# Turning the gated attention output by DMA instead of on TensorE, with a new order of work in the attention groups

## The reference

```python
h = _layernorm(x) * (1 + ca) + sa
xn = h / norm(h) * scale * gamma                # _L0_attn_ref
q, kv, a = split(einsum('bnd,ed->bne', xn, W_qkva), 3)
a = sigmoid(a)
y = scan over n:  y[n] = a[n] * y[n-1] + kv[n]
x = x + ga * (q * y)
h = _layernorm(x) * (1 + cb) + sb
x = x + gb * fp4_linear(silu(fp4_linear(h, w_gate)) * fp4_linear(h, w_up), w_down)
```

## Time and profile before

| | before |
|---|---|
| median of 3 executions | 1963.17 us |
| the profiled execution | 1961.58 us |
| its span, first to last instruction | 1959.8 us |
| busy in the span: TensorE | 1936.3 us (99%) |
| VectorE | 1686.6 us (86%) |
| ScalarE | 629.5 us (32%) |
| GpSimd | 1198.9 us (61%) |
| mean granted TensorE clock | 0.998 of full speed |

### The profile page before, as it was taken

How to read it: one execution, slowest core, us unless ns; L and a number is a source line. 1 busy time by engine, 2 the same in 40 slices (tenths; PEclk the granted TensorE clock), 3 DMA queues, 4 the chain that set the end, 5 groups by cost and what they waited for, 6 DMA issues and landing times.

```text
span 1959.8 us, 27185 instructions
## 1 busy us (share of the span) xinstructions
PE 1936.3 (99%) x9403; PEld 927.2 (47%) x9403; DVE 1686.6 (86%) x2106; ACT 629.5 (32%) x885; POOL 1198.9 (61%) x1072
## 2 busy tenths in 40 slices
PE   8999999999999999999999999999999999999998
PEld 3444444444444444444444444444444444444444
DVE  7786767676868999999999999999999999999986
ACT  4333433343413233233233323323232332322221
POOL 1554764546535777677667667767766776776641
PEclk9999999999999999999999999999999999999999
DMA  8866665757552433433433343343334334333323
GB/s 292 272 178 144 174 170 149 174 142 200 125 129 69 108 74 80 98 75 72 92 89 72 81 100 74 74 94 88 73 84 96 72 76 97 80 72 87 88 62 77
DMA packets 421251, 218.22 MB, mean 111 GB/s; under 512 B 359858, under 2 KB 359870, under 8 KB 421188
## 3 DMA queue, kind: packets, MB, share of 16 engines
q1 hardware_dynamic: 421188, 217.39, 45.1%
HBM read 95.43 MB, written 33.57 MB: 66 GB/s over the span
## 4 chain that ended last, share of the span: by engine, by line
PE 87%; DVE 6%; issue 2%; POOL 2%; DMA 1%; ACT 1%; SPq 1%; DVEq 0%; POOLq 0%
PE bank L1067 43%; PE bank L986 20%; PE bank L1087 15%; PE bank L1091 7%; PE bank L1011 1%; SPq L398 1%; DVE arena L1163 1%; DMA arena<-arena 1%; DVE bn L1152 1%; DVE arena L1292 0%; DMA arena<-in_L_attn_x_dram 0%; DVE arena L1454 0%; PE bank L925 0%; DMA arena<-in_L_ffn_w_up_dram 0%; DVE arena L1461 0%
## 5 line engine op out<-in xcount | busy, mean ns | idle before, releaser
L1067 PE MATMUL bank<-wgu_hi,arena 128*128 128x512 f16 (+1 forms) x3072 | 869.9, 362 | 2.0 <-DVE arena L1401 2.0
L1067 PE MATMUL bank<-wgu_lo,arena 128*128 128x512 f16 (+1 forms) x1536 | 555.7, 362 | 0.0
L986 PE MATMUL bank<-arena,wq_hi 128*128 128x512 f16 x1536 | 458.5, 380 | 2.3 <-DMA arena<-arena 1.3
L1067 PEld LDWEIGHTS bank<-wgu_hi,arena 128*128 128x128 f16 x3072 | 300.5, 98 | 310.1 <-issue 2.4
L986 PE MATMUL bank<-arena,wq_lo 128*128 128x512 f16 x768 | 292.3, 381 | 0.0
L1087 PE MATMUL bank<-wd_hi,arena 128*128 128x512 f16 x693 | 263.0, 379 | 0.1
L1087 PE MATMUL bank<-wd_lo,arena 128*128 128x512 f16 x693 | 263.0, 380 | 0.0
L986 PEld LDWEIGHTS bank<-arena,wq_hi 128*128 128x128 f16 x1536 | 150.0, 98 | 178.4 <-issue 3.7
L1067 PEld LDWEIGHTS bank<-wgu_lo,arena 128*128 128x128 f16 x1536 | 150.2, 98 | 153.7
L663 POOL TENSOR_TENSOR arena<-arena 128x512 f32<-128x512 f32 x63 | 153.2, 2431 | 95.4 <-DVE arena L1476 95.4
L1401 DVE SCALAR_TENSOR_TENSOR arena<-bank,small,arena 128x512 f32<-128x512 f32 (+1 forms) x192 | 134.1, 701 | 85.8 <-PE bank L1067 81.5
(11 more groups left out here) (162 smaller groups left out, 2743.6 us busy)
## 6 DMA issues: line engine op xcount, KB each, us to landing
arena<-in_L_attn_x_dram SPq DMA_DIRECT2D x32, 1024.0 KB, 5.9
arena<-x_scratch SPq DMA_DIRECT2D x128, 256.0 KB, 3.2
x_scratch<-arena SPq DMA_DIRECT2D x16, 1024.0 KB, 4.4
out_dram<-arena SPq DMA_DIRECT2D x64, 256.0 KB, 3.1
arena<-in_L_wmod_dram SPq DMA_DIRECT2D x6, 1024.0 KB, 14.4
arena<-arena SPq DMA_TRANSPOSE x258, 3.5
wgu_hi<-in_L_ffn_w_gate_dram SPq DMA_DIRECT2D x1, 2816.0 KB, 12.3
wgu_lo<-in_L_ffn_w_up_dram SPq DMA_DIRECT2D x1, 2816.0 KB, 19.0
```

The source lines that it names most:

```text
L986: last = pe.matmul(dst[m % 2][:, :].rearrange("p (j t) -> p j t", j=NJ), w[:, k, at], uT[p][:, half, :, k, :], start=(n == 0), stop=(n == ...
L1067: last = pe.matmul(dst[n][:, 0:w], xT[p][:, half, k, :], wt[:, k, cut], start=(m == 0), stop=(m == 3 * KD - 1))
```

## The change

The mix product is no longer turned on TensorE. VectorE writes it over the decay buffer (float32, channels on partitions). ScalarE copies it as 16-bit integers into two planes, the low and the high half of each float32 (`split_mix`, 1024 elements an instruction, four a group). When the four chunks of a group are split, SP issues one DMA transpose of 32 blocks of 128x128 16-bit elements (`turn_mix`). ScalarE puts the planes together again into float32 rows (`join_mix`, one instruction for each of the four row blocks), and `add_x` reads these from SBUF instead of PSUM. The state is kept in two buffers instead of four, and its last column is copied into a small `carry` tile after each scan.

```diff
+                def turn_mix(i):
+                    sp.wait_ge(mix_split, CH * (i + 1))
+                    wait(sp, mix_joined, NJ * i)
+                    sp.dma_start(mixT_bits..., mix_bits..., transpose=True).then_inc(mixT_loaded, 16)
...
                 def decays(i, m):
                     act.wait_ge(a_ready, CH * i + m + 1)
-                    wait(act, state_ready, CH * i + m - 1)
+                    wait(act, mix_split, CH * i + m - 1)
...
+                def split_mix(i, m):
+                    act.wait_ge(mix_ready, CH * i + m + 1)
+                    wait(act, mixT_loaded, 16 * i)
+                    act.activation(mix_bits[:, :, :, m, :], decay[m % 2].bitcast(U16)..., ACT.Copy).then_inc(mix_split, 1)
+
+                def join_mix(i, js):
+                    act.wait_ge(mixT_loaded, 16 * (i + 1))
+                    for j in js:
+                        wait(act, x1_ready, NJ * i + j - 1)
+                        act.activation(mix_rows[j % 2].bitcast(U16)..., mixT_bits[:, :, j, :]..., ACT.Copy).then_inc(mix_joined, 1)
...
                 def mix(i, p, b, m, first):
+                    if not first:
+                        dve.wait_ge(carry_ready, CH * (i - 1) + m + 1)
-                    dve.tensor_tensor_scan(state[m], ..., 0.0 if first else state[m][:, GT - 1:GT], ...)
+                    dve.tensor_tensor_scan(state[m % 2], ..., 0.0 if first else carry[:, m:m + 1], ...)
+                    dve.tensor_copy(carry[:, m:m + 1], state[m % 2][:, GT - 1:GT]).then_inc(carry_ready, 1)
-                    dve.scalar_tensor_tensor(mixT[p][:, m, :], q_bank[m % 2][:, :], ...)
+                    dve.scalar_tensor_tensor(decay[m % 2], q_bank[m % 2][:, :], ...)
...
-                        dve.tensor_tensor(xr[:, j, :], t_bank[j % 2][:, :], xr[:, j, :], ALU.add)
+                        dve.tensor_tensor(xr[:, j, :], mix_rows[j % 2], xr[:, j, :], ALU.add)
```

More of the change, by code:

```diff
@@ L176, in adaln_block_kernel @@
         used[0] -= B * KD * P + CH * B
-        state = [view(GT) for _ in range(CH)]
+        state = [view(GT) for _ in range(2)]
+        mix_rows = [view(D) for _ in range(2)]
         xs[0] = view(NJ * D).rearrange("p (j d) -> p j d", j=NJ)
@@ L846, in group @@
-                    decays(i, 1)
-                    if more:
-                        squares(i + 1, 1 - p, (2, 3))
-                        u_hi(i + 1, 1 - p)
-                    else:
+                        decays(i, 1)
+                        split_mix(i, 0)
+                        weights(0)
+                        join_mix(i - 1, (2, 3))
                         steps_of_x(0, 0)
                         x_hi(0, 0)
+                        weights(1)
+                        decays(i, 2)
@@ new lines, in group @@
+                        split_mix(i, 1)
+                        weights(2)
+                        ffn_apply(2, 0)
+                        steps_of_x(1, 1)
+                        decays(i, 3)
+                        split_mix(i, 2)
+                        x_hi(1, 1)
+                        ffn_apply(3, 1)
+                        weights(3)
+                        return
+                    squares(i + 1, 1 - p)
+                    u_hi(i + 1, 1 - p)
+                    join_mix(i - 1, (0, 1))
@@ L865, in group @@
+                    weights(2)
+                    decays(i, 3)
+                    split_mix(i, 2)
                     weights(3)
                 groups(group)
+                split_mix(NGA - 1, 3)
                 silu(0, 0, 0, 0)
@@ L881, in tile @@
                         x_hi(3, 1)
+                        join_mix(NGA - 1, range(NJ))
                         return
@@ L1286, in finish_modulation @@
                                            ALU.mult))
+                carry = col("gamma_q", KD)
                 def mix(i, p, b, m, first):
@@ L1514, in group @@
                     mix(i, p, b, 0, first)
+                    if not more:
+                        add_x(i - 1, (0, 1))
+                        first_stats(0)
+                        first_stats(1)
+                        finish_modulation()
+                        weights(0)
+                        add_x(i - 1, (2, 3))
+                        mix(i, p, b, 1, first)
+                        quantise_x(0, 0)
+                        first_stats(2)
+                        x_lo(0, 0)
+                        weights(1)
+                        mix(i, p, b, 2, first)
+                        weights(2)
+                        quantise_x(1, 1)
+                        mix(i, p, b, 3, first)
+                        x_lo(1, 1)
+                        first_stats(3)
+                        weights(3)
+                        return
+                    if two_more:
+                        stats_mean_var(i + 2, p)
                     add_x(i - 1, (0, 1))
+                    u_lo(i + 1, 1 - p)
+                    mix(i, p, b, 1, first)
+                    weights(0)
+                    add_x(i - 1, (2, 3))
                     if i == 1:
@@ L1518, in group @@
                         weight_max(3, raw_down[1])
-                    if not more:
-                        first_stats(0)
-                        first_stats(1)
-                        finish_modulation()
-                    weights(0)
-                    add_x(i - 1, (2, 3))
-                    mix(i, p, b, 1, first)
-                    if two_more:
-                        stats_mean_var(i + 2, p)
-                    if more:
-                        u_lo(i + 1, 1 - p)
-                    else:
-                        quantise_x(0, 0)
-                        first_stats(2)
-                        x_lo(0, 0)
-                    if i == 1:
                         diagonal(t_bank[0], wmax_turned, wmax_diagonal)
@@ L1541, in group @@
                     weights(2)
-                    if not more:
-                        quantise_x(1, 1)
                     mix(i, p, b, 3, first)
-                    if not more:
-                        x_lo(1, 1)
-                        first_stats(3)
                     weights(3)
@@ L1606, in tile @@
                         x_lo(3, 1)
+                        add_x(NGA - 1, range(NJ))
                         return
```

96 lines of the change are left out of this document (47 added, 49 removed).

## The result

The changed kernel takes 2023.0 us (median of 4 runs, 2022.4 to 2025.7), beside 1963.3 for the kernel before on the same chip: ratio 1.031, 95% interval 1.0289 to 1.0325. The forecast was 1986, the range 1966 to 2006. The direction was right, the size was not. The profiled execution took 2025.7, its span is 2023.9.

A forecast was written before the change was run, and what follows sets the result against it. TensorE, busy 1936.3 of 1959.8 us, was taken as the bound. Delays of 15.3 by group 15, 7.3 at attention's end and 1.5 in the FFN made 24.1 on 1961.58: 1985.7, said as 1986, range 1966 to 2006.

The forecast's parts named there:

- From group 7 on ... no wait. So groups 7 to 14 each win 1.74: Steady attention groups: TensorE never waits, so each group saves its two transpose batches, 1.74 us.
- 1.5 lost: Groups 11 to 14: w_down tiles 1408 wide instead of 1024 eat 2 us of slack; 1.5 us lost.
- Mix(i,1) was put at T + 21: Steady groups, T being the group's start on TensorE: second mix product done at about T+21, needed by T+23.3.
- Joins, store and x's load were put at T + 14, T + 26 and T + 30: Steady groups, after group start T: joins done by T+14, store at T+26, xr load at T+30.
- an add 0.65: VectorE's chain to mix(i,1): one add_x addition between the joins and u_lo takes 0.65 us.
- The store's landing, 4.35 in the text: SP's queue: the store and its landing take 4.35 us, from 164.52 to 168.87 in the profile before.
- Group 15: Last attention group: joins end T+15.5, TensorE waits 7.3 us for mix(15,1), first FFN tile begins about T+40.2.
- In the FFN 1.5 were put: FFN tiles 0 and 1: two transpose batches go, but VectorE's chain to tile 1's hidden product is no shorter; 1.5 lost.
- Groups 1 to 6: Early groups: TensorE waits, chiefly 9.7 us in group 1, 4.1 and 11.3 in group 4, 5.1 in group 5.
- Transfer: Mix's 32-block DMA transpose: lands 7 us after issue, bounds 3.6 and 12.4.
- The slow-transfer rival: The 32 blocks need 12.4 us; groups 7 to 14 wait 20 in all, group 1 4 more: 2008 us, chance 0.15.
- if groups 7 to 14 still wait, the slow transfer or the copies hold: Sign for two rivals: 12.4 us transfer (2008, chance 0.15) or 16-bit copies at double cost (1999, chance 0.12).

The follow-up runs named there:

- e12: Changed kernel with GpSimd's dequantise, from group 6 on, waiting for the four additions of add_x, VectorE's order untouched: 2006.2 us.
- e3: Changed kernel with the two additions add_x(i-1,(2,3)) ahead of the weight's rounding on VectorE instead of behind it: 1998.2 us.
- e4: Changed kernel with group 1's two w_down weight maxima on VectorE moved from behind add_x(0,(2,3)) to behind the statistics: 2017.4 us.
- e1: Changed kernel with each group's next weight load and turns ahead of the wait for x1's store in SyncE's queue: 2033.3 us.

## Why the prediction was wrong

The profiled span is 64.1 us longer (2023.9 against 1959.8), the sum said 24.1. The 40 missing:

- **"From group 7 on ... no wait. So groups 7 to 14 each win 1.74" failed**: 25.7 us. Groups 7 to 9 win 0.2 to 0.5 each, groups 10 to 14 lose 1.7 to 3.7: some 17 of the 25.7 us lie in groups 11 to 14, where the w_down tiles, 1408 wide, go through the same loops and the text counted 1.5 lost. It walked this very chain, but as dates against TensorE's, and did not see it as a loop. Mix(i,1) was put at T + 21 and came at T + 24.5 in group 8. Joins, store and x's load were put at T + 14, T + 26 and T + 30; they came at T + 19.1, T + 29.9 and T + 35.2.
- **The term that was mis-sized is add_x**, "an add 0.65", taken from before, where one input came from PSUM. After, both are in SBUF, and beside GpSimd two take 3.02 us, 3.68 in group 12. Closed into a loop, the text's own terms (7.0 + 2.1 + 0.65 + 2.74 + 2.2 + 2.44 + 1.29 + 4.35 + 0.4 + 6.0) give 29.2 us, 1.9 under TensorE's 31.09: closing it would not by itself have shown the loss. It took 32.2. The two additions brought 1.8 of the difference, the store's landing 0.9, x's load with the weight's loads and turns 0.7 (7.1 instead of 6.4); transfer and mix gave back 0.5. Without the stretch the loop is 30.5, and e12, which takes the stretch away, runs groups 7 and 8 at 31.1. e3 and e12 put 17 to 25 us on it.
- The store's landing, 4.35 in the text, was 5.3; x's next load now leaves right behind it. In groups 1 to 12 it is 5.1 to 5.5; in groups 13 to 15 of the same run, where no such load is left, 4.3. No run moves the load alone.
- **Group 15**: put at T + 40.2, came at T + 45.8: 5.7 us. TensorE's wait was 12.5, not 7.3; mix's transfer, behind the w_down turns, left at T + 10.7 and the joins ran from T + 18.5 to T + 20.7, where the text had them ended at T + 15.5. In the FFN 1.5 were put and 7.2 lost: 5.7 us (waits of 5.0 and 2.5, the first 34 us after its start).
- Groups 1 to 6 missed 3.0 us by the start of group 7: waits of 10.8 (9.7), 7.0 (4.1), 10.1 (11.3) and 5.2 (5.1). Transfer 6.8 (7), copies 1.05 and 1.16 (1.06), carry copies 0.15: right. Here the mechanism held, as e4 shows once more.
- The slow-transfer rival, which came closest in time (2008), was wrong in its cause. By its own terms it is 2010 (1986 + 20 + 4), and the forecast, with the 1.6 us that it names, 1987.
- The named sign "if groups 7 to 14 still wait, the slow transfer or the copies hold" was wrong too: they waited, and both were as forecast.

## What to carry to other kernels

When an operand moves from PSUM to SBUF, look at what GpSimd does beside the instruction: the same pair of additions cost 1.28 us or 3.0 to 3.7. Where each round of a pipeline waits for a transfer that the last one issued, sum the loop once around, with every queue in it, and hold that against the bottleneck's period. If it fits by a few per cent only, as here 29.2 in 31.1, price its terms as they run beside the others, for that margin is smaller than what they grow by. And a queue's order goes with the engines' orders: the same orders on VectorE and ScalarE cost 108 us or 17, by SyncE's order alone.

## What was not expected of the hardware

- Two 128x512 additions with both inputs in SBUF: 1.28 us alone, 3.02 beside a GpSimd multiply over 128x1024, 3.68 beside one over 128x1408; with one input in PSUM 1.28 beside the former. The second of the two ends 0.5 us after the multiply does.
- The 32-block transfer lands 6.7 to 7.9 us after issue in groups 2 to 15 of the changed kernel. In e1, where a 1 MB load has left just ahead of it, it takes 9.1 to 11.1 in 13 of these 14 groups (9.13 us of the 11.1 in issuing).
